# Order and size of SyncE's transfers in the two attentions of a fused two-layer kernel

## What is computed

```python
    x = L0_attn_x
    xn = _layernorm(x, axis=-1)
    s = _L0_attn_ref(xn, ...)          # 16 heads of 8, causal, relu on q, k and v, layer norm
    g = _silu(_L0_ffn_ref(xn, ...))
    x = x + s * g
    xn = _layernorm(x, axis=-1)
    s = _L1_attn_ref(xn, L1_attn_w_q, L1_attn_w_k, L1_attn_w_v, L1_attn_w_o)
    g = _silu(_L1_ffn_ref(xn, ...))    # 8 experts, the best 2 per token
    x = x + s * g

    # in _L1_attn_ref
    a = jnp.einsum('nhtd,nhsd->nhts', q, k) / jnp.sqrt(jnp.asarray(dk, x.dtype))
    a = jnp.where(mask[None, None], jnp.asarray(-jnp.inf, a.dtype), a)
    a = jax.nn.softmax(a, axis=-1)
    y = jnp.einsum('nhts,nhsd->nthd', a, v)
```

## Time and profile before

| | us |
|---|---|
| median of three runs | 3143.34 (3133.44 to 3148.9) |
| the profiled execution | 3142.21 |
| its span in the trace | 3140.4 |
| TensorE busy | 2492.1 (79%) |
| VectorE busy | 2154.0 (69%) |
| GpSimd busy | 1582.3 (50%) |
| ScalarE busy | 1471.2 (47%) |

### The profile page before, as it was taken

The page is one execution under the profiler, slowest core; times in us unless marked ns, Lnnn a source line. Parts: engine busy times, 40 slices in busy tenths (PEclk is TensorE's granted clock), DMA queues, the critical chain, the costliest instruction groups (busy, mean ns, idle before and its releaser), DMA issues. The chain is left out here.

```text
span 3140.4 us, 58914 instructions
## 1 busy us (share of the span) xinstructions
PE 2492.1 (79%) x19217; PEld 1524.0 (49%) x19231; DVE 2154.0 (69%) x5288; ACT 1471.2 (47%) x2463; POOL 1582.3 (50%) x1686
## 2 busy tenths in 40 slices
PE   0025459999898996689999999968869999999996
PEld 0013323333333332656666666648855565556664
DVE  8988637887887886356666666636646676777674
ACT  3444415555555554144445454436644444444442
POOL 4546521231322211057777777744426676767675
PEclk9987759999999998589999999979989999999998
DMA  2030031322223131101111111123221122112212
GB/s 54 0 126 0 3 99 54 103 79 83 88 73 102 63 100 39 67 19 47 39 45 40 47 40 43 44 86 84 83 58 39 53 60 60 52 52 60 60 46 59
DMA packets 203167, 184.27 MB, mean 59 GB/s; under 512 B 39680, under 2 KB 166721, under 8 KB 202946
## 3 DMA queue, kind: packets, MB, share of 16 engines
q1 hardware_dynamic: 194768, 164.86, 17.4%
q0 software_dynamic: 8192, 16.79, 1.8%
HBM read 105.65 MB, written 69.60 MB: 56 GB/s over the span
## 5 line engine op out<-in xcount | busy, mean ns | idle before, releaser
L1896 DVE CUSTOM_DVE_ANT_0 a_scored<-a_pMax,a_causal 128x128 bf16<-128x128 f32 (+3 forms) x1024 | 450.3, 485 | 448.1 <-PE a_pMax L2051 428.6
L1022 DVE TENSOR_REDUCE a_max<-a_pair_banks 128x2 f32<-128x1024 f32 (+3 forms) x512 | 406.5, 821 | 168.3 <-PE a_pair_banks L636 98.7
L1807 ACT ACTIVATE a_PT<-a_pST 128x1024 f32<-128x1024 f32 (+1 forms) x384 | 339.0, 883 | 389.4 <-PE a_pST L2041 377.1
L956 ACT ACTIVATE a_PT<-a_pair_banks 128x1024 f32<-128x1024 f32 (+1 forms) x384 | 337.0, 884 | 332.8 <-PE a_pair_banks L636 195.4
L1732 POOL TENSOR_SCALAR_AFFINE_SELECT a_PT<-a_PT 128x256 f32<-128x256 f32 x512 | 203.9, 410 | 359.2 <-ACT a_PT L1807 331.2
L2059 PE MATMUL a_pO<-a_PT,a_V 128*64 128x512 f32 (+3 forms) x2048 | 328.9, 466 | 1.4 <-POOL a_PT L1732 1.4
L890 POOL TENSOR_TENSOR a_att<-a_att,a_rows 128x512 f32<-128x512 f32 x16 | 20.3, 1268 | 564.5 <-DVE a_att L1086 564.5
L1750 POOL TENSOR_TENSOR a_SM<-a_PT 128x768 f32<-128x768 f32 x128 | 235.1, 1837 | 10.7
L2059 PEld LDWEIGHTS a_pO<-a_PT,a_V 128*64 128x64 f32 x2048 | 142.9, 144 | 172.7 <-issue 138.4
L2034 PE MATMUL a_pST<-a_q_high,a_k_high 64*128 64x512 f32 (+3 forms) x1024 | 200.0, 387 | 28.4 <-ACT a_PT L1807 28.3
L2041 PE MATMUL a_pST<-a_max_rows,a_ones_rows 64*128 64x512 f32 (+3 forms) x1024 | 152.5, 335 | 60.1 <-DMA a_max_rows<-a_mT 60.1
(11 more groups left out here) (330 smaller groups left out, 6457.5 us busy)
## 6 DMA issues: line engine op xcount, KB each, us to landing
a_rden<-inverse_sums_dram SPq DMA_DIRECT2D x256, 128.0 KB
a_KS<-k_parts_dram SPq DMA_DIRECT2D x64, 224.0 KB
a_QS<-q_parts_dram SPq DMA_DIRECT2D x64, 192.0 KB
m_x<-x_sorted_dram SPq DMA_DIRECT2D x71, 128.0 KB, 2.3
y_sorted_dram<-m_y SPq DMA_DIRECT2D x71, 128.0 KB, 1.8
x_sorted_dram<-ffn_zeros SPq DMA_DIRECT2D x17, 512.0 KB, 5.1
a_max_rows<-a_mT SPq DMA_DIRECT2D x512, 2.0 KB
q_parts_dram<-a_parts SPq DMA_DIRECT2D x16, 384.0 KB, 2.6
```

The source lines that it names most:

```text
L956: a.activation(PT[p][:, :, at:at + w], score_bank[k][:, :, 0:w], ACT.Exp, scale=SCALE).then_inc(exped.sem, 1)
L1022: last = v.tensor_reduce(MX[:, :, p, j], max_bank[m][:, :, at:at + (j + 1) * P], AX.X, ALU.max, negate=True)
L1807: a.activation(PT[s.q % 2][:, :, k * TOK:k * TOK + w], pST[:, :, 0:w], ACT.Exp, scale=SCALE).then_inc(exped.sem, 1)
L1896: last = v.tensor_tensor_reduce(scored[:, cc, at:at + w], pMax[:, cc, at:at + w], causal[:, TOK - w:], -1.0, 3e38, ALU.add, ALU.min, MX[pa ...
```

## The change

SyncE's order: in both attentions `m_rows` is called ahead of the other transfers of a step or unit; in the first attention that moves it ahead of `put_q` in odd units, in the second ahead of `inverses` and `sums_compact`. In the second attention `m_rows` issues two transfers of two rows in place of four of one, and `inverses` two broadcasts in place of four, each to 64 partitions and both pairs. The thresholds of the waits follow: 32 in place of 64.

```diff
                     elif not n.no_before:
                         store_x1(b - 1, 1 - n.parity)
-                    if n.prepare:
-                        put_q(b + 2)
                     if not n.end:
                         m_rows(u + 1, (s + 1) % 4 // 2, (s + 1) % 2)
                     if n.prepare:
+                        put_q(b + 2)
                         put_k(b + 2)
...
                 for h in range(2):
-                    for k in range(2):
-                        at = (2 * h + k) * TB
-                        sp.dma_start(MQ[i][DH * h + k:DH * h + k + 1, :].bitcast(F32), mT[at:at + TB, :].bitcast(F32)).then_inc(m_put, 16)
+                    sp.dma_start(MQ[i][DH * h:DH * h + 2, :].bitcast(F32), mT[MR * h:MR * (h + 1), :].bitcast(F32)).then_inc(m_put, 16)
...
-                for h in range(4):
-                    row = rden_d.rearrange("(h o q) -> h o q", h=4, o=1)[h]
-                    sp.dma_start(RB[DH * (h % 2):DH * (h % 2) + DH, h // 2, :], row.to_broadcast([DH, TOK])).then_inc(broadcast, 16)
+                for h in range(2):
+                    of_pairs = rden_d.rearrange("(n h o q) -> h o n q", n=2, h=2, o=1)[h]
+                    sp.dma_start(RB[DH * h:DH * h + DH, :, :], of_pairs.to_broadcast([DH, 2, TOK])).then_inc(broadcast, 16)
...
+                    if s.turn_m:
+                        m_rows(s.r + 1, (q + 1) % 2)
                     if s.invert:
                         inverses(s.g - 1)
                     if s.sums:
                         sums_compact(s.g - 1)
-                    if s.turn_m:
-                        m_rows(s.r + 1, (q + 1) % 2)
...
-                    a.wait_ge(m_put, 64 * r)
+                    a.wait_ge(m_put, 32 * r)
...
-                v.wait_ge(broadcast, 64 * (g + 1))
+                v.wait_ge(broadcast, 32 * (g + 1))
...
-                    pe.wait_ge(m_put, 64 * (s.r + 1))
+                    pe.wait_ge(m_put, 32 * (s.r + 1))
```

## The result

| | kernel before | changed kernel |
|---|---|---|
| median of the runs, us | 3139.9 (4 runs, 3133.4 to 3148.9) | 3023.9 (4 runs, 3016.5 to 3033.5) |
| ratio, 95% interval | | 0.9619, 0.9572 to 0.9665 |
| profiled execution, us (its span) | 3142.2 (3140.4) | 3020.3 (3018.5) |
| granted clock over the span | 0.923 | 0.927 |

The change gained 116 us by these medians, 121.9 us by the two spans. The forecast was 101 us, 3042; 3023.9 lies in its range of 3022 to 3072, but at the very end of it, and the profiled execution, 3020.3, just outside.

The account below looks back on a forecast made before the run. The prediction took TensorE to bound the kernel, standing in even steps of the second attention for the rows of maxima. Terms of 70 + 20 + 10 + 1 = 101 us took 3143 to 3042 us, range 3022 to 3072.

Parts of the forecast that it names:

- (a): Second attention, even steps: sending the rows of maxima first, in two transfers, removes TensorE's whole wait for them, 70 us.
- The bound of 86.6 us: Upper bound on TensorE's wait for the rows' transfer in the second attention, from the records of its weight loads.
- (b): Second attention: TensorE's clock no longer falls behind 14 of those stalls, 20 us; bounds -5 and 29.
- the low clock moves house: Rival: TensorE's waits for VectorE in part two take over the clock's falls; 3052 to 3067 us, chance 0.12.
- the floor of the pair: Sign in the second attention: even steps of 10.9 us, an even and odd step together about 21.5 in its first part.
- (c): First attention: rows ahead of the q transfers in odd units let TensorE start earlier, 10 us; bounds 0 and 12.
- (d): Second attention, end of each part: inverse sums in two broadcasts instead of four, 1 us; range 0 to 2.4.
- The wait changes hands: Rival: in even steps TensorE waits for VectorE's low part of k instead; 3067 to 3090 us, chance 0.10.
- It isn't the rows: Rival: the waits are wrongly put down to the rows' transfer; 3131 to 3143 us, chance 0.03.
- slower: Rival: merged transfers of rows land late, over few DMA engines; over 3159 us, chance 0.03.

Follow-up runs that it names:

- before_again: The kernel before, unchanged, run and traced again beside the changed kernel and its parts: 3148.9 us, ratio 1.0002.
- first_te_unrolled: The changed kernel with the first attention's eight turns written out on TensorE instead of partly looped: 3065.3 us, ratio 0.9755; repeated, 3039.1 us, 0.9658.
- sets A and E: Groups of kernels run in turn on one chip beside the kernel before; the changed kernel, unaltered, took 3065.6 us in E (0.9745).
- B, C, D and F: Other such groups of runs beside the kernel before; the changed kernel, unaltered, had 0.9629 in B and 0.9609 in C.
- mixing_in_gaps: The changed kernel with part 1's whole mixing of experts moved into VectorE's gaps in even steps, ScalarE's tanh one step earlier: 3068.7 us, ratio 0.9763.
- te_padded: The changed kernel with 24 already met waits ahead of TensorE's second-attention steps in both parts, moving its later code: 3031.6 us, ratio 0.9639.
- before_longer_odd: The kernel before with the second round's first pair of matmuls done four times in every odd step of the second attention: 3138.7 us, ratio 0.9972.

## Why the prediction was right or wrong, point by point

**What bounds the kernel.** Right: TensorE, and in even steps its wait for the rows. The wait goes whole, by the order alone.

**(a) The wait, 70 us.** Right in mechanism and, on its own trace, in size: the delays of L2041 beyond 0.80 us add up to 70.9 us before and 1.0 after. The bound of 86.6 us was no bound: in before_again the same wait is 90.7 us above what the changed kernel has, counted in the same way, and the gain is the same.

**(b) The clock, 20 us.** Mis-sized by little. 14 even steps of before lasted 25.0 us too long at a low clock, none after. Part 1's waits for VectorE made it fall in four odd steps, as they did before, so nothing was given back: 25 is what the term measured, and "the low clock moves house" did not happen: of 14 waits of 1.3 us for VectorE four ended in a step of 12.9 us instead of 11.7. The Trainium skill, page "TensorE: Matmul & The Clock Gate", section "HAM oscillation — how this bites in real kernels", tells of half clock in each round with a wait for a transfer, a longer one than these; here it was fewer than one in three.

**The step that failed** is the floor of the pair, "a pair of steps about 21.5 in part one". It came as 20.9 us (10.77 + 10.12). The forecast took the odd step's 10.67 us as its own length. 0.55 of that was lateness, and its mark stood in the trace of before as the wait for the exponential, 28.3 us, which the forecast didn't read. From step 5 of each part on the odd steps add up to 630.0 us before and 612.4 after: 17.6 us. Even steps are 10.77 us and not the 10.89 that the forecast had from 12.68 - 1.79, 6 us more: a delay of L2041 lengthens its step by 0.1 us more than itself. With the 70 of (a) and the 25 of (b) that is 119 us, and the second attention gained 118.3. The forecast's 90 for it left out 24. Since the lateness came with the trace of before and not with that of after, the odd steps' part of the difference isn't the change's alone: a late trace of before stands against free runs of after. Free of the lateness the kernel before is no faster, as before_again shows; its wait for the rows is 20.8 us longer instead. So in free runs it is term (a) that is larger, 90.7 us where the forecast had 70. In a late set the change gains 2.55% (0.9745), 81 us; in free ones 3.7 and 3.9%, 118 and 127 us by the medians.

**(c) The first attention, 10 us.** Wrong. 1.0001 for that part alone, with an interval that reaches 0.15% down, 5 us. The step that failed is the reading of the surplus: "fits the rows' landing" was a coincidence in time at borders that come every 100 us, once per turn of four units. first_te_unrolled takes the surplus away and leaves the rows where they are in the changed kernel. It is the loop's jump on TensorE.

**(d) The broadcasts, 1 us.** Nil: 4.83 us from the first issue to VectorE before, 4.69 after in part 1, and 5.22 in part 0. With the same bytes in half as many transfers SyncE was free earlier, and the data were no sooner there. The forecast had named that as its lower end.

**Rivals.** "The wait changes hands": no; the wait of L2070 for the low part of k is 1.1 us in four times. "It isn't the rows" and "slower": no.

**The sum.** 101 was forecast and 121.9 came by the spans: +5 in (b), +24 in the floor, -8 in (c), -1 in (d), together +20. That the total missed by only 20 is in part luck: 9 us of errors in (c) and (d) stand against 29 in (b) and the floor. In a late set 81 came, and the forecast would have been too high. Its range holds both medians, 3023.9 and 3065.6, but it was made for neither case: it knew nothing of the lateness.

## What to carry to other kernels

When a wait is to be removed, ask to what the thing waited for is tied. Here the landing of the rows hung on the start of the step before, so that step's own length cost nothing until the wait was gone, and everything after: measure the steps that lean on the wait as if they counted in full, and read every wait in them, even one that costs nothing today. A surplus that comes back at equal distances points to the loop before it points to a transfer. And before a gain is read from two traces, one kernel should be traced in both sets.

## What the runs showed of the hardware

TensorE can end groups of matmuls 0.7 to 1.1 us later than usual (1.4 in a single step), nearly always at one place (the second round of an odd step, straight behind the 16 matmuls of L2056), at a granted clock of 1.00 and with recorded starts that don't differ; both engines that wait for these groups start late. It came and went with the set of runs: sets A and E, and the first trace of before; not B, C, D and F, of which F ran on the chip of A. Five programs were seen both ways. Where and how much it shows goes with the program: 0.7 to 0.8 us in some odd steps with the rows sent last, 1.0 to 1.1 in nearly all with the rows sent first. Even that has an exception: in mixing_in_gaps part 1's steps 3 and 7 were late, and steps 1 and 5, behind the grown ones, took 10.1 to 10.25 us. What it is stays open; the code's address (te_padded, in a set free of it) wasn't tried in a late set.

A jump back in TensorE's loop cost 1.1 to 3.4 us of idle time at each of five borders of the first attention, though VectorE, the last that it waited for, was done. It isn't a price of every jump: TensorE's loop in the second attention jumps five times in each part too, and the steps across those jumps take 10.11 to 10.15 us in part 0 of the changed kernel, like its other odd steps.

Added work can be free: 32 us of it on TensorE cost before_longer_odd nothing, since it stood in place of a wait; in the changed kernel, without that wait, the same work cost 20 to 28 us.
